# A transformer block on one core: ten units of QKV ahead and spilled, successive slots, turning by DMA, fp16 state

## The chip, the cores and the metric

The kernel runs on one core of a Trainium2 chip. Its time is the device time of one launch in microseconds, the median of several runs.

## What is computed

x has 4 sequences of 1024 tokens of 512 values. The reference, cut:

```python
x = x + layernorm(attn(layernorm(x)))
x = x + layernorm(ffn(layernorm(x)))

def attn(x):                       # 16 heads of 32, chunks of 128 tokens
    q, k, v = heads(x @ w_qkv.T + b_qkv)
    for each chunk:                # the state S is 32 x 32 a head
        inter  = (q * decay_q) @ S
        intra  = ((q @ k.T) * dmask) @ v
        S      = lam_c * S + (k * decay_k).T @ v
    return (inter + intra) @ w_out.T + b_out

def ffn(x):                        # weights rounded to fp8 e4m3
    return (silu(x @ gate * gate_s) * (x @ up * up_s)) @ down * down_s
```

## The kernel before

The tokens go in 16 units of 256 (two tiles of 128, `t`, or two chunks, `c`). Every wide product is made of fp16 halves: a number is a high half (written by ScalarE) and a low half (the number less the high half, written by GpSimd or VectorE), and three (two where the weights are rounded) fp16 matmuls are added in PSUM.

Each engine has its own program, written out by hand as a list of calls, and semaphores order them. `start` does unit 0's attention, unit 1's QKV and all the weights' preparation: VectorE rounds 12 pieces of 128x1536 to fp8 values (`magic`, L915 and L917; `rounded`, L922 and L924), and TensorE sums their squares (L496). Then `slot(s)` does three things at once: attention and out-projection of unit s, FFN of unit s-1, QKV of unit s+1. Slots 1 to 14 are of this kind; slot 15 has no QKV, slot 16 only the FFN of unit 15. A sequence is four units.

A slot on TensorE, in order (`slot`, L646): x1 of unit s-1 turned by 8 f32 transposes (L654); scores (L552), carry (query times state, f32, L565) and state (f32, L569) of chunk 0; gate and up (`gate_up`, L513) in six steps of 32 matmuls, with the other scores, `attend` (L583, L585), chunk 1's carry and state, and the turning of the next x (L441) between them; QKV's q and k (L621) with the turning of o (L595); out-projection (L603), down (L528) and V (L635); the turning of k (L644). PSUM banks, q and k (f32) and the state stay in place from one user to the next.

SyncE's list (`slot`, L274): load of the next x, stores, and `stack` (L253), which puts high and low halves of q and k on top of each other in `stacks` by 32 copies within SBUF (L261). GpSimd's list: low halves of the probabilities (L771), of h (L758), of q and k (L776) and of v (L784), the inverse standard deviations (L709, L712), the residuals (L793, L805), the decay of the f32 state of 128x512 (L765).

## Time and profile before

| | us |
|---|---|
| median of 3 runs (lowest, highest) | 1132.33 (1130.96, 1132.65) |
| the profiled execution | 1132.8 |
| its span | 1131.0 |
| TensorE busy | 1046.4 |
| VectorE, GpSimd, ScalarE busy | 733.5, 585.1, 391.6 |

The span runs from the first to the last profiled instruction. Busy times are of the span; matmuls overlap, so a block of them is best read as the distance from its start to the next block's start. A slot is the distance from one turning of x1 to the next.

### The profile page before, as it was taken

The numbers are of one execution on the slowest core, as the hardware profiler recorded it, in microseconds if no ns is written. First come the engines' busy times: TensorE is split into PE (matmuls) and PEld (weight loads), VectorE is DVE, ScalarE is ACT, GpSimd is POOL, SyncE is SP. The second block draws the span as 40 slices with busy tenths as digits, with TensorE's granted clock in tenths as the row PEclk, the third lists the DMA queues.
The fourth block names the chain that finished last, engine by engine and source line by source line (L and its number), as shares of the span: only waits on it lengthen the run. The fifth ranks groups of instructions, "written<-read, shape, count | busy, mean of one in ns | idle before, by whom it ended". The sixth has DMA issues, their size and how long they took to land.

```text
span 1131.0 us, 23001 instructions
## 1 busy us (share of the span) xinstructions
PE 1046.4 (93%) x8772; PEld 792.4 (70%) x8772; DVE 733.5 (65%) x1427; ACT 391.6 (35%) x752; POOL 585.1 (52%) x647
## 2 busy tenths in 40 slices
PE   1738689999999999999999999999999999999887
PEld 1537277786959687786959596786959596877654
DVE  7979984757657474756657474757667484746642
ACT  3324244251524233252424243342514243342211
POOL 0123454655656474655647474645556464656433
PEclk9867889999999999999999999999999999999989
DMA  9311501303040312213040312213040402112000
GB/s 364 105 65 57 122 1 36 77 16 89 11 103 12 69 45 50 66 22 82 11 103 11 74 39 55 61 27 77 13 101 11 86 28 59 55 38 58 1 19 19
DMA packets 83626, 66.09 MB, mean 58 GB/s; under 512 B 9280, under 2 KB 70848, under 8 KB 83392
## 3 DMA queue, kind: packets, MB, share of 16 engines
q1 hardware_dynamic: 82656, 64.00, 21.8%
q8 instruction: 75, 1.23, 0.5%
q10 hardware_dynamic: 864, 0.61, 0.2%
q14 instruction: 31, 0.25, 0.1%
HBM read 24.72 MB, written 8.39 MB: 29 GB/s over the span
## 4 chain that ended last, share of the span: by engine, by line
PE 84%; DVE 12%; issue 2%; POOL 1%; DMA 0%; POOLq 0%; ACT 0%; DVEq 0%; SPq 0%
PE bank L513 30%; PE bank L528 14%; PE bank L621 13%; PE bank L603 7%; PE bank L635 6%; PE bank L565 3%; PE bank L569 2%; PE bank L552 2%; PE bank L583 2%; DVE ffn_pool L922 2%; PE bank L654 1%; PE bank L441 1%; PE bank L644 1%; PE bank L595 1%; DVE ffn_pool L915 1%
## 5 line engine op out<-in xcount | busy, mean ns | idle before, releaser
L771 POOL TENSOR_TENSOR att_pool<-p,att_pool 128x512 f16<-128x512 f32 x128 | 148.1, 1178 | 80.8 <-ACT att_pool L371 80.8
L513 PE MATMUL bank<-ffn_pool,gate_q 128*128 128x256 f16 x1536 | 185.1, 274 | 3.8 <-DVE ffn_pool L1194 3.8
L513 PE MATMUL bank<-ffn_pool,up_q 128*128 128x256 f16 x1536 | 184.6, 274 | 0.0
L621 PE MATMUL bank<-x_hl,wqkv_hi 128*128 128x256 f16 x1024 | 171.3, 274 | 14.1 <-DVE wqkv_lo L906 14.1
L528 PE MATMUL bank<-down_q,ffn_pool 128*128 128x512 f16 x768 | 170.6, 379 | 1.0 <-DVE ffn_pool L1084 1.0
L513 PEld LDWEIGHTS bank<-ffn_pool,gate_q 128*128 128x128 f16 x1536 | 148.8, 98 | 21.5 <-DVE ffn_pool L1194 4.2
L513 PEld LDWEIGHTS bank<-ffn_pool,up_q 128*128 128x128 f16 x1536 | 151.0, 98 | 18.1
L758 POOL TENSOR_TENSOR ffn_pool<-ffn_pool 128x512 f16<-128x512 f32 x96 | 111.1, 1157 | 94.4 <-ACT ffn_pool L385 92.9
L371 ACT CAST att_pool<-p 128x512 f16<-128x512 f32 x128 | 77.9, 618 | 191.7 <-DVE p L1074 191.7
L1084 DVE SCALAR_TENSOR_TENSOR ffn_pool<-bank,us_t,ffn_pool 128x256 f32<-128x256 f32 x192 | 84.1, 480 | 89.4 <-PE bank L513 87.3
L621 PE MATMUL bank<-x_hl,wqkv_lo 128*128 128x256 f16 x512 | 140.5, 274 | 0.0
L528 PEld LDWEIGHTS bank<-down_q,ffn_pool 128*128 128x128 f16 x768 | 75.1, 98 | 91.6 <-DVE ffn_pool L1084 1.3
L776 POOL TENSOR_TENSOR att_pool<-qk,att_pool 128x512 f16<-128x512 f32 x60 | 71.1, 1186 | 116.0 <-ACT att_pool L351 116.0
L621 PEld LDWEIGHTS bank<-x_hl,wqkv_hi 128*128 128x128 f16 x1024 | 99.2, 98 | 27.5 <-issue 15.0
L357 ACT CAST v_hl<-v 128x512 f16<-128x512 f32 x32 | 19.8, 619 | 253.1 <-DVE v L1147 253.1
L1074 DVE TENSOR_TENSOR p<-bank,mask 128x512 f32<-128x512 f32 x128 | 83.5, 684 | 33.6 <-POOL att_pool L771 33.6
L379 ACT ACTIVATE ffn_pool<-bank,gs_t 128x256 f32<-128x256 f32 x192 | 80.3, 468 | 64.7 <-PE bank L513 64.7
L603 PE MATMUL bank<-wout_hl,o_t 128*128 128x512 f16 x384 | 91.6, 391 | 5.4 <-DVE o_t L1141 5.4
L709 POOL TENSOR_TENSOR rstd<-mv,eps_t 128x1 f32<-128x1 f32 (+1 forms) x112 | 23.3, 208 | 139.0 <-DVE mv L982 139.0
L346 ACT ACTIVATE qk<-bank,bqk 128x256 f32<-128x256 f32 x128 | 53.7, 470 | 89.9 <-PE bank L621 89.9
L635 PE MATMUL bank<-wqkv_hi,x_hl 128*128 128x512 f16 x256 | 76.1, 379 | 0.0
L1158 DVE SCALAR_TENSOR_TENSOR y<-bank,o_scale,bo 128x512 f32<-128x512 f32 x32 | 23.9, 748 | 80.5 <-PE bank L603 80.5
(123 smaller groups left out, 1658.9 us busy)
## 6 DMA issues: line engine op xcount, KB each, us to landing
att_pool<-att_pool SPq DMA_DIRECT2D x480, 64.0 KB, 2.1
x_t<-in_x SPq DMA_DIRECT2D x16, 512.0 KB, 3.5
out_x<-ffn_pool SPq DMA_DIRECT2D x32, 256.0 KB, 2.1
att_pool<-in_w_qkv_t SPq DMA_DIRECT2D x4, 768.0 KB, 8.1
ffn_pool<-in_gate_w SPq DMA_DIRECT2D x4, 768.0 KB, 12.9
ffn_pool<-in_up_w SPq DMA_DIRECT2D x4, 768.0 KB, 4.2
ffn_pool<-in_down_w SPq DMA_DIRECT2D x4, 768.0 KB, 4.6
mask<-in_mask_c SPq DMA_DIRECT2D x1, 1024.0 KB, 17.0
```

The lines of the kernel that those rows point to most:

```text
L371: nc.scalar.copy(pr_hl[:, 0, heads(s, g)], by_head(p32[:, g % 2])).then_inc(p_hi_d, 1)
L379: ins = nc.scalar.activation(sil[:, j], b_gate[:, j * TOK:(j + 1) * TOK], ACT.Silu, scale=gs_t[:, 2 * i + j:2 * i + j + 1])
L513: ins = nc.tensor.matmul(b[:, j * TOK:(j + 1) * TOK], w[:, k, o * P:(o + 1) * P], x1_hl[:, part, k], start=(k == 0 and part == 0), stop=(k ...
L528: ins = nc.tensor.matmul((b_gate, b_up)[t][:, :], h_hl[:, part, k, t * P:(t + 1) * P], down_q[:, k], start=(k == 0 and part == 0), stop=(k ...
L603: ins = nc.tensor.matmul((b_y, b_att)[c][:, :], o_t[:, c, a, k], wout_hl[:, b, k], start=(k == 0 and n == 0), stop=(k == KT - 1 and n == 2))
L621: ins = nc.tensor.matmul(b_t[i % 2][:, j * TOK:(j + 1) * TOK], (wqkv_hi, wqkv_lo)[a][:, k, o * P:(o + 1) * P], x_hl[:, b, k], start=(k == ...
L635: ins = nc.tensor.matmul(b_t[t][:, :], x_hl[:, b, k, t * P:(t + 1) * P], (wqkv_hi, wqkv_lo)[a][:, k, 2 * D:3 * D], start=(k == 0 and q == ...
L758: nc.gpsimd.tensor_tensor(h_hl[:, 1, 2 * i:2 * i + 2].rearrange("p k t -> p (k t)"), h32[:, i % 2], h_hl[:, 0, 2 * i:2 * i + 2].rearrange( ...
L771: nc.gpsimd.tensor_tensor(pr_hl[:, 1, heads(s, g)], by_head(p32[:, g % 2]), pr_hl[:, 0, heads(s, g)], ALU.subtract).then_inc(p_lo_d, 1)
L776: nc.gpsimd.tensor_tensor(qk_hl[:, 1, 2 * i:2 * i + 2].rearrange("p k t -> p (k t)"), qk[:, 2 * i:2 * i + 2].rearrange("p k t -> p (k t)") ...
L1074: nc.vector.tensor_tensor(by_head(p32[:, g % 2]), by_head(b_s[g % 2][:, :]), mask[:, heads(s, g)], ALU.mult).then_inc(p_d, 1)
L1084: ins = nc.vector.scalar_tensor_tensor(out=h32[:, i % 2, j * TOK:(j + 1) * TOK], in0=b_up[:, j * TOK:(j + 1) * TOK], scalar=us_t[:, 2 * i ...
```

## The change

- **QKV ahead.** `LEAD = 10`: the QKV products of units 0 to 9 are made first (`ahead(k)`), the other six in slots 0 to 5 (unit s+10 in slot s). Fp16 halves of q, k, v and of v times its decay go to DRAM (`spill_qk`, `spill_v`) and are loaded a slot before their use (`load_stacks`, `load_kt`, `load_v`). The rounding of the weights (`ROUNDED`) runs beside units 0 to 7.
- **Successive slots.** Slot s has the attention of unit s, the out-projection of unit s-1 (and its norms, residual, x1), the FFN of unit s-2. There are 18 slots. Slots 0 and 1 have no FFN (`early`), slots 6 to 15 no QKV, slots 16 and 17 no attention. The loop over sequences is written out.
- **Turning by DMA.** x, o, x1 and k are turned as fp16 halves by DMA transposes that SyncE issues: 128 rows of 1024 fp16 numbers (256 KB) each, two for x, o and x1, one of 512 KB for k. The f32 transposes on TensorE, and the PSUM copies behind them, go. Low halves of x and x1 are now made by GpSimd (two instructions of 128x512 each), also v times its decay and its low half (two each).
- **Fp16 state.** The state is 128x4x32, is scaled and split into halves (`state_scaled`, `state_hi`, `state_lo`), sent to DRAM and read back stacked in four pieces (`move_state`) before the next chunk's carry. Carry is 16 fp16 matmuls of 32 columns, state 12 of 128 columns.

```diff
...
+        dram_qk = nc.dram_tensor("dram_qk", [units, 2, 2, KT, P, TOK], F16, kind="Internal").ap()
+        dram_v = nc.dram_tensor("dram_v", [units, T, P, 4 * D], F16, kind="Internal").ap()
+        dram_s = nc.dram_tensor("dram_s", [2, P, 2 * P], F16, kind="Internal").ap()
...
+        ROUNDED = {0: (0,), 1: (1,), 2: (2, 3), 3: (4, 5), 4: (6,), 5: (7, 8), 6: (9,), 7: (10, 11)}
...
-                    for j in range(HG):
-                        for r in range(4):
-                            sp.dma_start(stacks[DH * r:DH * (r + 1), which, j::HG, :],
-                                         qk_hl[DH * j:DH * (j + 1), parts[r], KT * which:KT * (which + 1), :]
-                                         ).then_inc(done, 16)
...
+            def turn_o(s):
+                for t in range(T):
+                    sp.wait_ge(o_lo_d, 2 * s + t + 1)
+                    if t == 0:
+                        sp.wait_ge(*((out_mm, 2 * s) if s else (v_mm, 2 * LEAD)))
+                    sp.dma_start_transpose(turned(o_t[:, :, :, :].rearrange("p s k t -> p (s k) t"), t),
+                                           hl_1[:, t].rearrange("p s d -> p (s d)")).then_inc(o_turned, 16)
...
+            def spill_v(n, t):
+                sp.wait_ge(vd_lo_d, 2 * n + t + 1)
+                sp.dma_start(dram_v[n, t], vv[:, t]).then_inc(v_spilled[t], 16)
+
+            def load_stacks(s):
+                sp.wait_ge(q_spilled, 32 * (s + 1))
+                sp.wait_ge(k_spilled, 32 * (s + 1))
+                if s:
+                    sp.wait_ge(score_mm, 8 * s)
+                    sp.wait_ge(carry_mm, carries(s, 0))
...
+                for which, parts in ((1, (0, 0, 1, 1)), (0, (0, 1, 0, 1))):
+                    for r in range(4):
+                        sp.dma_start(stacks[DH * r:DH * (r + 1), which],
+                                     dram_qk[s, which, parts[r]].rearrange("g (j d) t -> d (g j) t", d=DH)
+                                     ).then_inc(stack_in, 16)
...
+            def load_v(s):
...
+                if s:
+                    sp.wait_ge(att_mm, 2 * s)
+                    sp.wait_ge(state_mm, states(s, 0))
...
+                sp.dma_start(vva, dram_v[s].rearrange("t p c -> p t c")).then_inc(v_in, 16)
+
+            def move_state(s, c):
+                if not has_state(s, c):
+                    return
+                n = states(s, c)
+                sp.wait_ge(state_lo_d, n + 1)
+                sp.dma_start(dram_s[n % 2], state_hl[:, :].rearrange("p s g e -> p (s g e)")).then_inc(state_out, 16)
+                sp.wait_ge(state_out, 16 * (n + 1))
+                at_least(sp, carry_mm, carries(s, c + 1) if has_carry(s, c) else carries(s, c))
+                for r in range(4):
...
+            for k in range(LEAD):
+                ahead(k)
+            load_stacks(0)
+            load_kt(0)
+            load_v(0)
...
+                if n < units:
+                    if s:
+                        turn_x(n)
+                    spill_v(n - 1, 0)
+                    spill_v(n - 1, 1)
+                    if n + 1 < units:
+                        load_x(n + 1)
...
+                if attends:
+                    move_state(s, 0)
+                if v >= 1:
+                    store(v - 1, 1)
+                if attends:
+                    load_xr(s)
+                if v < 0 and n < units:
+                    spill_qk(n, 0)
+                if s + 1 < units:
+                    load_stacks(s + 1)
+                    load_kt(s + 1)
+                if 0 <= u < units:
+                    turn_x1(u)
+                if attends:
+                    move_state(s, 1)
+                if s + 1 < units:
+                    load_v(s + 1)
...
+                if attends:
+                    turn_o(s)
...
+            def carry_and_state(s, c):
+                if c == 0:
+                    pe.wait_ge(v_d, 2 * min(units, LEAD + s))
+                    pe.wait_ge(kt_in, 16 * (s + 1))
+                    pe.wait_ge(v_in, 16 * (s + 1))
...
+                if has_carry(s, c):
+                    pe.wait_ge(state_in, 64 * states(s, c))
...
+            def slot(s):
+                n, u, v = s + LEAD, s - 1, s - 2
+                attends, projects = s < units, u < units
+                if attends:
+                    scores(s, 0, 0)
+                    carry_and_state(s, 0)
+                gate_up(v, 0)
+                if projects:
+                    project(u, 0)
+                    project(u, 1)
+                if attends:
+                    scores(s, 0, 1)
+                gate_up(v, 1)
+                gate_up(v, 2)
+                if attends:
+                    attend(s, 0)
+                    scores(s, 1, 0)
+                gate_up(v, 3)
+                if attends:
+                    scores(s, 1, 1)
+                    carry_and_state(s, 1)
+                gate_up(v, 4)
+                gate_up(v, 5)
+                if attends:
+                    attend(s, 1)
+                down(v, 0)
+                if n < units:
+                    for i in range(4):
+                        project_qk(n, i)
+                    project_v(n, 0)
+                    project_v(n, 1)
+                down(v, 1)
...
```

**Place 1: VectorE and GpSimd while QKV runs ahead.** VectorE before, in `start` (`v` is the sum of V and its bias, `gate_q` a rounded piece, `small` maxima):

```order
L922 TENSOR_TENSOR ffn_pool<-ffn_pool 128x1536
L924 TENSOR_TENSOR gate_q<-ffn_pool 128x1536
L915 TENSOR_SCALAR ffn_pool<-ffn_pool 128x1536
L917 TENSOR_SCALAR ffn_pool<-ffn_pool 128x1536
L1147 TENSOR_TENSOR v<-bank,bv 128x512 x2
L922 TENSOR_TENSOR ffn_pool<-ffn_pool 128x1536
L924 TENSOR_TENSOR gate_q<-ffn_pool 128x1536
L915 TENSOR_SCALAR ffn_pool<-ffn_pool 128x1536
L917 TENSOR_SCALAR ffn_pool<-ffn_pool 128x1536
```

VectorE now, in `ahead(2)`:

```order
L1154 TENSOR_SCALAR ffn_pool<-ffn_pool 128x1536
L1158 TENSOR_TENSOR ffn_pool<-ffn_pool 128x1536
L1160 TENSOR_TENSOR gate_q<-ffn_pool 128x1536
L1221 TENSOR_SCALAR xr<-xr,mv,rstd 128x512 x2
L1152 TENSOR_SCALAR ffn_pool<-ffn_pool 128x1536
L1154 TENSOR_SCALAR ffn_pool<-ffn_pool 128x1536
L1158 TENSOR_TENSOR ffn_pool<-ffn_pool 128x1536
L1160 TENSOR_TENSOR gate_q<-ffn_pool 128x1536
L1237 TENSOR_TENSOR v<-bank,bv 128x512 x2
```

GpSimd now, in `ahead(2)` (`qk_hl`, `vv`, `hl_x` are low halves, L897 multiplies v by its decay):

```order
L886 TENSOR_TENSOR qk_hl<-qk,qk_hl 128x512
L895 TENSOR_TENSOR vv<-v,vv 128x16x32
L897 TENSOR_TENSOR v<-v,decay_k 128x512
L886 TENSOR_TENSOR qk_hl<-qk,qk_hl 128x512
L895 TENSOR_TENSOR vv<-v,vv 128x16x32
L897 TENSOR_TENSOR v<-v,decay_k 128x512
L864 TENSOR_TENSOR rstd<-mv,eps_t 128x2
L867 TENSOR_TENSOR rstd<-rstd,eps_t 128x2
L886 TENSOR_TENSOR qk_hl<-qk,qk_hl 128x512
L901 TENSOR_TENSOR vv<-v,vv 128x512 x2
L886 TENSOR_TENSOR qk_hl<-qk,qk_hl 128x512
L881 TENSOR_TENSOR hl_x<-xr,hl_x 128x512 x2
```

The same rounding now stands between the norms of x, and 12 GpSimd instructions of 512 columns stand beside each unit of QKV.

**Place 2: SyncE in a slot.** Before, a slot of the loop (x of the next unit, the store, the stacking of q, then of k):

```order
L277 ISA [waits x1_d]
L277 DMA x_t<-in_x 128x2x512
L266 REGISTER_ALU
L267 ISA [waits fin_d]
L267 DMA out_x<-ffn_pool 128x512
L271 ISA
L256 ISA [waits stored]
L261 DMA att_pool<-att_pool 32x4x256 [waits qk_lo_d,qk_hi_d]
L261 DMA att_pool<-att_pool 32x4x256 x15
L261 DMA att_pool<-att_pool 32x4x256 [waits qk_lo_d,qk_hi_d]
L261 DMA att_pool<-att_pool 32x4x256 x15
```

Now, slot 4, its first part (turning of x, spill of v, load of x, `move_state(4, 0)` in L345 and L350, store, x for the residual):

```order
L278 DMA_TRANSPOSE x_hl<-hl_x 128x8x128 [waits v_mm,x_lo_d]
L278 DMA_TRANSPOSE x_hl<-hl_x 128x8x128 [waits x_lo_d]
L307 DMA dram_v<-vv 128x2048 [waits vd_lo_d] x2
L268 DMA x_q<-in_x 128x2x512 [waits x_lo_d]
L345 DMA dram_s<-state_hl 128x256 [waits state_lo_d]
L350 DMA state_st<-dram_s 32x4x128 [waits carry_mm,state_out]
L350 DMA state_st<-dram_s 32x4x128 x3
L362 DMA out_x<-ffn_pool 128x512 [waits fin_d]
L358 DMA xr<-in_x 128x2x512 [waits fin_d]
```

and its second part (stacks, k, x1, `move_state(4, 1)`, v, o):

```order
L319 DMA att_pool<-dram_qk 32x16x256 [waits score_mm,carry_mm,k_spilled,q_spilled]
L319 DMA att_pool<-dram_qk 32x16x256 x7
L327 DMA_TRANSPOSE kt<-dram_qk 128x2x1024 [waits state_mm]
L295 DMA_TRANSPOSE ffn_pool<-hl 128x8x128 [waits up_mm,x1_lo_d]
L295 DMA_TRANSPOSE ffn_pool<-hl 128x8x128 [waits x1_lo_d]
L345 DMA dram_s<-state_hl 128x256 [waits state_lo_d]
L350 DMA state_st<-dram_s 32x4x128 [waits carry_mm,state_out]
L350 DMA state_st<-dram_s 32x4x128 x3
L338 DMA vv_pool<-dram_v 128x2x2048 [waits att_mm,state_mm,v_spilled1,v_spilled0]
L287 DMA_TRANSPOSE o_t<-hl 128x8x128 [waits out_mm,o_lo_d]
L287 DMA_TRANSPOSE o_t<-hl 128x8x128 [waits o_lo_d]
```

The loads of the next unit and the turning stand in one list with the two trips of the state.

**Place 3: GpSimd ahead of the spill of v.** Before, the end of slot 1 (L784 are the low halves of v, in the slot that projects them):

```order
L793 TENSOR_TENSOR x<-x_t,y 128x512
L709 TENSOR_TENSOR rstd<-mv,eps_t 128x1
L712 TENSOR_TENSOR rstd<-rstd,eps_t 128x1
L709 TENSOR_TENSOR rstd<-mv,eps_t 128x1
L712 TENSOR_TENSOR rstd<-rstd,eps_t 128x1
L805 TENSOR_TENSOR ffn_pool<-x,ffn_pool 128x512
L709 TENSOR_TENSOR rstd<-mv,eps_t 128x1
L712 TENSOR_TENSOR rstd<-rstd,eps_t 128x1
L793 TENSOR_TENSOR x<-x_t,y 128x512
L709 TENSOR_TENSOR rstd<-mv,eps_t 128x1
L712 TENSOR_TENSOR rstd<-rstd,eps_t 128x1
L784 TENSOR_TENSOR v_hl<-v,v_hl 128x16x32 x2
```

Now, slot 3, up to the low halves of the decayed v of unit 12 (`vd_lo`, L901), which SyncE's L307 waits for (L953 and L939 residuals, L933 probabilities, L947 h):

```order
L953 TENSOR_TENSOR ffn_pool<-xr,ffn_pool 128x512
L864 TENSOR_TENSOR rstd<-mv,eps_t 128x1
L867 TENSOR_TENSOR rstd<-rstd,eps_t 128x1
L933 TENSOR_TENSOR att_pool<-p,att_pool 128x512 x2
L947 TENSOR_TENSOR ffn_pool<-ffn_pool 128x512
L939 TENSOR_TENSOR xr<-xr,y 128x512 x2
L864 TENSOR_TENSOR rstd<-mv,eps_t 128x1
L867 TENSOR_TENSOR rstd<-rstd,eps_t 128x1
L947 TENSOR_TENSOR ffn_pool<-ffn_pool 128x512
L864 TENSOR_TENSOR rstd<-mv,eps_t 128x1
L867 TENSOR_TENSOR rstd<-rstd,eps_t 128x1
L901 TENSOR_TENSOR vv<-v,vv 128x512 x2
```

V's low halves move from the end of their slot into the next slot, behind the third low half of h.

## Rows read from the trace of the kernel before

**Rows 1.** The page: busy time and share of the span; the main DMA queue.
```profile
PE 1046.4 (93%) x8772; PEld 792.4 (70%) x8772; DVE 733.5 (65%) x1427; ACT 391.6 (35%) x752; POOL 585.1 (52%) x647
q1 hardware_dynamic: 82656, 64.00, 21.8%
```

**Rows 2.** Windows: us, busy of PE, PEld, DVE, ACT, POOL (instructions), PEclk, DMA share, GB/s.
```profile
27.70:146.00 118.30, 75.85 (x483) 52.28 (x481) 108.50 (x129) 37.81 (x49) 40.68 (x33) 0.75 0.29 84
463.80:526.90 63.10, 63.07 (x545) 48.27 (x546) 38.65 (x83) 22.85 (x46) 34.47 (x40) 1.00 0.22 52
```

**Rows 3.** Windows, TensorE only (us, busy, PEclk, DMA share, GB/s), block by block.
```profile
463.83:464.75 0.92, 0.92 (x8) 1.00 0.10 29
464.75:465.20 0.45, 0.45 (x11) 1.00 0.00 0
465.20:466.14 0.94, 0.94 (x11) 1.00 0.00 0
466.14:467.18 1.04, 1.04 (x11) 1.00 0.03 8
467.18:470.68 3.50, 3.50 (x33) 1.00 0.02 5
478.11:478.99 0.88, 0.88 (x35) 1.00 0.73 272
500.06:505.30 5.24, 5.24 (x51) 1.00 0.20 41
505.30:507.88 2.58, 2.58 (x14) 1.00 0.50 102
507.88:513.07 5.19, 5.19 (x26) 1.00 0.50 101
```

**Rows 4.** Timeline, TensorE: the first QKV matmuls (start, length, idle before).
```profile
23.75 0.58 PE L621 MATMUL bank<-x_hl,wqkv_hi 128*128 128x256 f16 x2 [12.96 <-DVE wqkv_lo L906]
```

**Rows 5.** Single lines: duration min/median/max in ns.
```profile
L776 POOL TENSOR_TENSOR att_pool<-qk,att_pool x60: 1152/1156/2057, 105.2 to 1011.6; 128x512 f16<-128x512 f32 x60
L985 DVE TENSOR_SCALAR nrm<-x_t,mv,rstd x32: 537/540/1371, 7.7 to 986.8; 128x512 f32<-128x512 f32 x32
```

**Rows 6.** Timeline, GpSimd and VectorE in the same stretch.
```profile
111.09 2.05 POOL L776 TENSOR_TENSOR att_pool<-qk,att_pool 128x512 f16<-128x512 f32 x1 [2.11 <-ACT att_pool L351]
113.71 2.06 POOL L776 TENSOR_TENSOR att_pool<-qk,att_pool 128x512 f16<-128x512 f32 x1 [0.57 <-ACT att_pool L351]
110.37 1.75 DVE L922 TENSOR_TENSOR ffn_pool<-ffn_pool 128x1536 f32<-128x1536 f32 x1
112.15 2.60 DVE L924 TENSOR_TENSOR down_q<-ffn_pool 128x1536 f16<-128x1536 f32 x1
114.87 1.72 DVE L915 TENSOR_SCALAR ffn_pool<-ffn_pool 128x1536 uint32<-128x1536 uint32 x1
116.62 0.96 DVE L917 TENSOR_SCALAR ffn_pool<-ffn_pool 128x1536 f32<-128x1536 f32 x1
```

**Rows 7.** SyncE's issues L261 and landing of L261, then landing of L277.
```profile
L261 SPq DMA_DIRECT2D att_pool<-att_pool x480: 585/601/1908, 115.3 to 1027.2; - x160
DMA to landing us min/median/max: 2.0/2.1/5.0
DMA to landing us min/median/max: 3.4/3.5/4.4
```

**Rows 8.** Timeline, GpSimd in the steady slot: probabilities' low halves, an inverse deviation.
```profile
468.44 2.27 POOL L771 TENSOR_TENSOR att_pool<-p,att_pool 128x512 f16<-128x512 f32 x2 [4.47 <-ACT att_pool L371]
...
516.98 0.19 POOL L709 TENSOR_TENSOR rstd<-mv,eps_t 128x1 f32<-128x1 f32 x1 [2.33 <-DVE mv L982]
517.25 0.54 POOL L712 TENSOR_TENSOR rstd<-rstd,eps_t 128x1 f32<-128x1 f32 x1
```

**Rows 9.** The chain of waits at the end: start, length, what.
```profile
1088.51 24.01 PE bank L513 x192
1124.07 0.70 DVE ffn_pool L1179
```

1601 lines of the change are left out of this document (869 added, 732 removed).

## The prediction

> **What bounds the kernel now.** I read the page first, for the engine with the largest share: TensorE, 93% [rows 1]. Then the windows. From 27.7 to 146.0 us it is VectorE that is full (108.5 of 118.3 us) and TensorE works at a granted clock of 0.75; in a steady slot TensorE is busy 63.07 of 63.10 us at 1.00, with VectorE at 38.65 and GpSimd at 34.47 [rows 2]. So 14 slots are TensorE's own time, and the start is VectorE's rounding of weights. The chain of waits at the end has the FFN of unit 15 alone: 24.01 us for its gate and up (192 matmuls), and 6.9 us from the end of down (1124.07) to the span's 1131.0 [rows 9]. The change must be judged by what it takes from 63.1, and by the waits that its longer way through DRAM brings.
>
> **TensorE's work.** Per unit, four f32 turnings of about 0.9 us go: -3.6 (the stretch from 463.83 for one) [rows 3]. Carry and state, 0.94 and 1.04 in f32, twice a unit (3.8 with the second pair's shorter state, 0.9), become 16 matmuls of 32 columns (half of `attend`'s 32 in 0.88: 0.44) and 12 of 128 columns (8 take 0.45: 0.67), so 2.2: -1.6 [rows 3]. A slot with everything is then 63.1 - 3.6 - 1.6 = 57.9 us; of it QKV is 2 x 5.24 + 5.19 = 15.7, so a slot without QKV is 42.2. Sixteen units are 926 us; before they were 1010. This gain of 83 us and the start's idle time are what the waits below are set against.
>
> **Start.** The first QKV matmul stood at 23.75, behind the low half of the weights [rows 4]. Ahead of that VectorE loses two low halves of x and a first `magic` (some 3.1 us with L915 and L917 at 0.96 [rows 6]) and gains two moments of x (1 us beyond what a wait hid): 21.6.
>
> **Ten units ahead.** TensorE needs 15.7 us each. GpSimd has 12 instructions of 512 columns a unit at 1.16 [rows 5]: 13.9. VectorE rounds twelve pieces in units 0 to 7 (1, 1, 2, 2, 1, 2, 1, 2), each 0.96 + 0.96 + 1.75 + 1.76 = 5.4, and normalises twice a unit, 2 x 0.54 [rows 5, 6]. These do not run side by side. At 111.09 a GpSimd instruction of 1.16 takes 2.05 beside L922, L924 takes 2.60 in place of 1.76 beside it, and at 113.71 and 114.87 the same again (2.06, and L915 1.72 for 0.96): each waits for the other's end [rows 6]. So a unit takes 13.9 + 1.1 + 5.4 per piece: 20.4 with one, 25.8 with two, 22.7 in unit 4, where the split of W_out (2048 columns, 2.3 at L922's pace) is added. Unit 0 has no V work and waits for the weights: 18; units 8 and 9 are TensorE's 15.7. Sum: 18 + 20.4 + 25.8 + 25.8 + 22.7 + 25.8 + 20.4 + 25.8 + 15.7 + 15.7 = 216. The bounds are 159 (no mutual waiting) and 240 (GpSimd idle 2 to 3 us a unit besides). The Trainium skill (SBUF — State Buffer, Who interferes with whom) counts a VectorE instruction with two SBUF inputs, as L922, as shut out by a GpSimd read too; L922's row beside GpSimd shows no stretch of its own, since it had begun first. If L922 were free of it, the stage would be 12 x 1.75 = 21 us shorter.
>
> **SyncE's list is the new path.** A plain copy costs SyncE 0.60 and lands in 2.1; one of 512 KB lands in 3.5, so 1 MB in about 5.1 [rows 7]. A turning is not in the trace. Its nearest rows are L261's: 0.60 as median, 1.91 as the longest; below 0.60 nothing excludes a little. I take 1.25, the middle, for 256 KB and 2.5 for k's 512 KB. The Trainium skill (Advanced Engine Details and Errata, X-Bar Transpose (TRN2)) has such DMAs as fast as plain ones; with 0.60 the sum below is some 13 us less. Against it stands the table in DMA: Bandwidth & Descriptors (Why a DMA increments its semaphore by 16 and not by 1): before the newest generation the issuing sequencer pushed one command a tile, 32 cycles each; with 64 tiles in a turning (16 rows by 128 numbers, my count) and SyncE's 1.2 GHz from the same skill that is 1.7 us and the fixed part, about 2 us, an estimate, and the sum is 30 us higher. No row here shows either.
>
> **The loads of the next slot (slots 7 to 15).** `load_stacks` may go once carry of chunk 1 has read the stacks. From there: 8 x 0.60 = 4.8, k 2.5, x1's turnings 2.5, the state out 0.4 + 2.1 and back 4 x 0.60 (4.9), v 0.4 + 5.1: 20.2 us. TensorE has left: state 0.7, two steps of 3.5, `attend` 0.9, down 10.4, the next scores 0.45: 19.4 [rows 3]. So v comes 0.8 late where chunk 1 has a state (7 of 9 slots).
>
> **The state within a slot (slots 2 to 6).** There SyncE can send the state of chunk 0 only after `spill_v`, which waits for `vd_lo`, late in GpSimd's list. GpSimd is through with the first probabilities at about 4.4 (before, at 470.71, 5.5 after the scores' end at 465.20, less the 1.3 of x1's low halves on VectorE, more 0.2 since down's eviction now stands first [rows 3, 8]). Up to the end of `vd_lo` stand 14 instructions of 1.16 (16.2), five inverse deviations of 0.8 (4.0), the state's two small ones and hand-overs (1.0 by estimate) [rows 5, 8]: 21.2, so 25.6. Then SyncE: 0.5 + 0.4 + 0.4, landing 2.1, 4 x 0.60, landing 2.1: 33.5. TensorE is at carry of chunk 1 at 0.45 + 1.1 + 3.5 + 5.2 + 0.45 + 7.0 + 0.9 + 0.45 + 3.5 + 0.45 = 23.0 [rows 3]. It waits 10.5. Queued behind carry are the rest of the FFN and QKV; VectorE and GpSimd wait for these. Bounds: 0 (GpSimd early) and 14.
>
> **Slots 0 to 2.** Slot 0: its stacks, k and v are asked for behind q and k of unit 9: casts 1.5 + 1.2, spills 1.2, stacks 4.8, k 2.5, v 5.5 = 16.7, against V's 5.2 and the scores: a wait of 11; the state's trip, as above, 9; work 21: 41. Slot 1: x of unit 11 is turned at the end of SyncE's list (4.8 + 2.5 + 4.9 + 0.4 + 1.2 + 2.5 + 2.5 + 2.1 = 20.9 after carry, TensorE has 5.7): 15.2; state 2.5; work 26.6: 44.3. Slot 2: v is 20.2 after carry, TensorE has 4.7: 15.5; state 9; work 57.9: 82.4.
>
> **The sum.** 21.6 + 216 + 41 + 44.3 + 82.4, slots 3 to 5 3 x 68.4 = 205.2, slot 6 42.2 + 10.5 = 52.7, slots 7 to 15 9 x 42.2 + 7 x 0.8 = 385.4, slot 16 (FFN, out-projection) 36.6, slot 17 31.4, the end 6.9: 1123.5. After long waits TensorE comes back at the lower clock: the last unit's gate and up took 24.01 where six steps of 3.50 are 21.0 [rows 3, 9]. Nine waits of 8 us or more, 3 us each: 27. That is 1150.5 as a span; the median of before lies 1.3 over the span of its profiled execution: **1152**. So the 83 us of work and some 20 at the old start are given back as waits.
>
> **Rivals.** (1) *The run-ahead goes at TensorE's pace*, 18 + 9 x 15.7 = 159, because GpSimd's and VectorE's instructions mostly miss each other. For it: GpSimd has 13.9 of 15.7 to do, and L776's median over 60 is 1.156. Against: most of those stood beside instructions that read PSUM; the two beside the rounding took 2.05 and 2.06 [rows 5, 6]. Time 1152 - 57 = 1095, faster. The point: if the ten units take under 196 us, the kernel is faster than before. (2) *Nothing waits*: besides, states and loads are there in time: 21.6 + 159 + 21 + 26.6 + 4 x 57.9 + 10 x 42.2 + 36.6 + 31.4 + 6.9 = 957. Against: the trip of the state is two landings and six issues long whatever GpSimd does. (3) *Turnings are dear*: each further us on SyncE adds 4 us in seven slots and 12 in slots 0 to 2, 40 in all; at 1.91, 1178, and with the clock lost in those seven slots 1195; at 2.5, 1220. (4) *The change turns its DMA engines into the bound.* 64 MB took 21.8% of 16 engines, 247 us [rows 1]; now a unit moves 8 to 9 MB, 33 us of a 58 us slot, and 3 MB, 12 us, per unit ahead. It would need twice that price; I count it with (3).
>
> **How the numbers follow.** Forecast 0.42 (1125 to 1175), (1) 0.22, (2) 0.07, (3) with (4) 0.24, of that 0.06 above 1240; the rest, 0.05, is partial cover between (1) and (2). The range 1075 to 1240 leaves out (2), the dearest turnings, and a little between. A measurement here tells 0.2% (2.3 us) from no change. Faster: (1), (2) and the rest, 0.34; same 0.03, from the forecast's lower end; slower 0.63.
>
> **What the new profile would show.** The tenth unit's V ending near 238, with GpSimd instructions of 2 us beside the rounding and TensorE idle in each of units 1 to 7; if near 180, (1) holds. In slots 3 to 6, one gap of about 10 us on TensorE ahead of carry of chunk 1, ended by a DMA into `state_st`; if none, the order on GpSimd was mis-read. In slots 8 to 15 gaps under 2 us ahead of the state matmuls; if 5 or more, turnings cost over 2 us. SyncE's transposes give their price directly. A slot without QKV of 42 us of busy time confirms the ledger. The forecast is wrong as a whole if the gaps ahead of carry are absent and the run-ahead is at TensorE's pace.

## The result

The changed kernel is slower, and by much more than forecast.

| | before | after |
|---|---|---|
| median, us | 1131.67 (4 runs) | 1273.45 (4 runs, 1269.99 to 1277.33) |
| after / before, 95% interval | | 1.1253 (1.1219 to 1.1287) |
| span of the profiled execution | 1131.0 | 1268.2 |
| forecast (range) | | 1152 (1075 to 1240) |

The forecast had 20 us more, the chip shows 142. The time lies outside the range. The lines of the page of after that answer to [rows 1], with the issues of SyncE's loads and their landing (KB each, median us):

```profile
PE 1003.2 (79%) x8500; PEld 711.6 (56%) x8500; DVE 679.1 (54%) x1227; ACT 431.0 (34%) x816; POOL 746.0 (59%) x830
...
q1 hardware_dynamic: 283184, 163.12, 52.5%
...
PE 44%; POOL 18%; issue 10%; SPq 8%; DVE 7%; ACT 6%; DMA 6%; POOLq 0%; DVEq 0%; ACTq 0%
...
att_pool<-dram_qk SPq DMA_DIRECT2D x128, 256.0 KB, 5.7
...
vv_pool<-dram_v SPq DMA_DIRECT2D x16, 1024.0 KB, 5.7
```

TensorE's work did fall, by 43 us of busy time, but it is busy 79% of the span and no longer 93%. The chain of what ended last, which was TensorE for 84% before, passes through GpSimd, SyncE and the DMAs for 32%. The bytes rose from 64 MB to 163.

By stage, windows of after (us, busy of PE, PEld, DVE, ACT, POOL, granted clock, DMA share, GB/s): ten units ahead, slots 0 to 2, slots 3 to 6, slots 7 to 15, and slot 8 alone, to be held against [rows 2].

```profile
22.70:278.30 255.60, 191.61 (x1236) 125.97 (x1236) 150.68 (x154) 111.55 (x192) 171.44 (x136) 0.86 0.51 151
278.30:482.40 204.10, 124.53 (x1092) 89.61 (x1091) 77.82 (x158) 59.48 (x115) 102.70 (x119) 0.77 0.65 152
482.40:753.30 270.90, 225.88 (x2000) 163.97 (x1998) 138.07 (x267) 92.61 (x181) 163.69 (x189) 0.92 0.51 120
753.30:1189.60 436.30, 392.51 (x3678) 283.19 (x3676) 268.47 (x565) 143.75 (x285) 271.99 (x336) 0.98 0.56 122
804.10:849.20 45.10, 42.62 (x402) 30.90 (x401) 29.74 (x65) 15.93 (x32) 30.83 (x40) 1.00 0.56 118
```

What TensorE waited for, in sum, times, longest (view of waits, TensorE):

```profile
PE bank L714 <- DMA state_st<-dram_s: 45.0, 6, 10.0
PE bank L714 <- issue: 43.6, 9, 12.0
PE bank L688 <- ACT qk L470: 34.4, 6, 9.5
PE bank L699 <- DMA att_pool<-dram_qk: 30.3, 3, 13.3
PE att L688 <- ACT qk L470: 27.2, 6, 6.9
```

L714 is carry, L688 V's product, L699 the scores. The second row, "issue", stands ahead of carry at a slot's start. TensorE's list waits there for V, the keys and the state, and it is the load of V that comes last: SyncE issues it at the end of the slot before. In slot 8 it was issued at 846.63 us, V's loads land 5.7 us after their issue (median), and slot 9's carry begins at 852.25. Where there is no second state to move, the wait is absent.

| stage | forecast | measured | of it waits |
|---|---|---|---|
| first QKV matmul | 21.6 | 22.7 | |
| ten units ahead | 216 | 255.6 | 61.6 ahead of V |
| slot 0, 1, 2 | 41, 44.3, 82.4 | 60.0, 57.8, 86.2 | 79.5 |
| slots 3 to 5 | 205.2 | 216.9 | 26.9 for the state |
| slot 6 | 52.7 | 54.0 | 7.4 for the state |
| slots 7 to 15 | 385.4 | 436.4 | 22.5 at the starts, 20.2 within |
| slots 16, 17, end | 74.9 | 78.6 | |
| clock after waits, as a lump | 27 | in the stages | |
| span | 1150.5 | 1268.2 | |

### The profile page after: what moved, and what is told of

The parts are those of the page before. It is cut to its first block, busy times and chain, and to the rows that moved or that the text cites. A ratio compares the mean times of both kernels' runs of the same rounds, so it can differ in the third digit from the quotient of the medians.

```text
span 1268.2 us, 21610 instructions
## 1 busy us (share of the span) xinstructions
PE 1003.2 (79%) x8500; PEld 711.6 (56%) x8500; DVE 679.1 (54%) x1227; ACT 431.0 (34%) x816; POOL 746.0 (59%) x830
## 3 DMA queue, kind: packets, MB, share of 16 engines
q1 hardware_dynamic: 283184, 163.12, 52.5%
## 4 chain that ended last, share of the span: by engine, by line
PE 44%; POOL 18%; issue 10%; SPq 8%; DVE 7%; ACT 6%; DMA 6%; POOLq 0%; DVEq 0%; ACTq 0%
PE bank L771 13%; PE bank L785 12%; PE bank L675 5%; PE att L748 5%; POOL att_pool L933 4%; PE bank L688 4%; POOL vv L895 3%; POOL v L897 3%; DMA dram_s<-state_hl 2%; SPq L319 2%; SPq L327 2%; POOL qk_hl L886 2%; DVE p L1243 2%; POOL vv L901 2%; PE att L675 2%
## 5 line engine op out<-in xcount | busy, mean ns | idle before, releaser
L771 PE MATMUL bank<-ffn_pool,gate_q 128*128 128x256 f16 x1536 | 196.7, 285 | 13.3 <-ACT ffn_pool L523 13.3
L933 POOL TENSOR_TENSOR att_pool<-p,att_pool 128x512 f16<-128x512 f32 x128 | 150.8, 1198 | 67.9 <-ACT att_pool L496 67.9
L771 PEld LDWEIGHTS bank<-ffn_pool,gate_q 128*128 128x128 f16 x1536 | 152.7, 102 | 42.2 <-ACT ffn_pool L523 20.0
L947 POOL TENSOR_TENSOR ffn_pool<-ffn_pool 128x512 f16<-128x512 f32 x96 | 111.2, 1158 | 97.9 <-ACT ffn_pool L529 97.9
L771 PEld LDWEIGHTS bank<-ffn_pool,up_q 128*128 128x128 f16 x1536 | 150.5, 98 | 22.5 <-DVE ffn_pool L1330 4.5
L675 PE MATMUL bank<-x_hl,wqkv_hi 128*128 128x256 f16 x704 | 124.6, 284 | 31.1 <-DVE wqkv_lo L1145 23.5
L496 ACT CAST att_pool<-p 128x512 f16<-128x512 f32 x128 | 76.9, 618 | 191.6 <-DVE p L1243 191.4
L785 PEld LDWEIGHTS bank<-down_q,ffn_pool 128*128 128x128 f16 x768 | 73.9, 98 | 99.2 <-DVE ffn_pool L1330 12.4
L886 POOL TENSOR_TENSOR qk_hl<-qk,qk_hl 128x512 f16<-128x512 f32 x64 | 80.2, 1256 | 83.1 <-ACT qk_hl L476 65.4
L864 POOL TENSOR_TENSOR rstd<-mv,eps_t 128x1 f32<-128x1 f32 (+1 forms) x112 | 27.9, 249 | 147.0 <-DVE mv L1218 136.6
L1243 DVE TENSOR_TENSOR p<-bank,mask 128x512 f32<-128x512 f32 x128 | 83.1, 681 | 50.1 <-PE bank L699 35.0
L529 ACT CAST ffn_pool<-ffn_pool 128x512 f16<-128x512 f32 x96 | 59.3, 617 | 128.9 <-DVE ffn_pool L1330 127.3
L675 PE MATMUL bank<-x_hl,wqkv_lo 128*128 128x256 f16 x352 | 99.8, 284 | 0.0
L675 PEld LDWEIGHTS bank<-x_hl,wqkv_hi 128*128 128x128 f16 x704 | 70.8, 102 | 46.8 <-issue 23.4
L688 PE MATMUL bank<-wqkv_hi,x_hl 128*128 128x512 f16 x176 | 64.6, 456 | 34.4 <-ACT qk L470 34.4
L714 PE MATMUL bank<-state_st,att_pool 128*128 128x32 f16 x448 | 15.8, 180 | 88.7 <-DMA state_st<-dram_s 45.0
L748 PE MATMUL att<-wout_hl,o_t 128*128 128x512 f16 x384 | 85.5, 379 | 0.0
L699 PE MATMUL bank<-att_pool 128*128 128x128 f16 x512 | 43.8, 226 | 40.6 <-DMA att_pool<-dram_qk 30.3
```

The costliest lines, as they stand in the source:

```text
L496: nc.scalar.copy(pr_hl[:, 0, heads(g)], by_head(p32[:, g % 2])).then_inc(p_hi_d, 1)
L675: ins = nc.tensor.matmul(qk_banks(n)[i % 2][:, j * TOK:(j + 1) * TOK], (wqkv_hi, wqkv_lo)[a][:, k, o * P:(o + 1) * P], x_mov(n)[:, b, k], ...
L688: ins = nc.tensor.matmul(qk_banks(n)[t], x_mov(n)[:, b, k, t * P:(t + 1) * P], (wqkv_hi, wqkv_lo)[a][:, k, 2 * D:3 * D], start=(k == 0 and ...
L748: ins = nc.tensor.matmul(b_y[t], o_t[:, a, k, t * P:(t + 1) * P], wout_hl[:, b, k], start=(k == 0 and n == 0), stop=(k == KT - 1 and n == 2))
L771: ins = nc.tensor.matmul(b[:, j * TOK:(j + 1) * TOK], w[:, k, o * P:(o + 1) * P], x1_hl[:, v % 2, part, k], start=(k == 0 and part == 0), ...
L785: ins = nc.tensor.matmul((b_gate, b_up)[t][:, :], h_hl[:, part, k, t * P:(t + 1) * P], down_q[:, k], start=(k == 0 and part == 0), stop=(k ...
```

## Experiments

All are the changed kernel with one or a few edits. Each row has two runs (four for `e30all` and `e96all`); the two of a kernel lie up to 7.9 us apart, so 4 us or less between kernels says nothing. The kernel before stood at 1131.3 to 1133.2 beside them. "Ahead" is the stage of the ten units, from the first QKV matmul to the last V.

| run | edit | us | against 1273.5 | ahead |
|---|---|---|---|---|
| e1 | ScalarE: fourth Q/K part first | 1250.7 | -22.8 | 228.9 |
| e2 | rounding left out | 1257.0 | -16.5 | 233.7 |
| e12 | both | 1220.4 | -53.1 | 195.7 |
| e18 | e1, and V's sum first on VectorE | 1246.3 | -27.1 | 227.2 |
| e20 | e18, and ScalarE's parts in a row | 1248.4 | -25.1 | 229.0 |
| e3 | state moved ahead of V's spill | 1264.9 | -8.6 | |
| e39 | e3, and half of the stacks from ScalarE | 1240.4 | -33.1 | |
| e37 | e3, and the FFN's input turned first | 1235.7 | -37.8 | |
| e4 | second key buffer from slot 6 on | 1255.3 | -18.1 | |
| e5 | unit 0's loads earlier | 1259.8 | -13.6 | |
| ekp | keys copied, not turned | 1263.8 | -9.6 | |
| epl | all turnings copies | 1256.2 | -17.3 | |
| e10 | half of the stacks' loads left out | 1227.7 | -45.8 | |
| e30 | stacks in 2 KB packets | 1271.6 | -1.9 | |
| eall | e1, e3, e4, e5, e37 | 1175.4 | -98.0 | 229.6 |
| eall2 | eall, e20's lists, earlier keys in slots 0, 1 | 1178.1 | -95.3 | 227.8 |
| e30all | eall and e30 | 1183.4 | -90.1 | 230.3 |
| e96all | eall, a quarter of the stacks' bytes less | 1159.9 | -113.6 | 230.3 |

### The ten units ahead

In after, TensorE stands ahead of the second half of V in units 0 to 8, for 4.2 to 9.5 us, and twice ahead of the first. Unit 4, timelines of ScalarE, VectorE, GpSimd and TensorE (start, length, idle before and what ended it):

```profile
149.67 0.62 ACT L486 CAST vv<-v 128x512 f16<-128x512 f32 x1 [5.56 <-POOL v L897]
153.56 0.62 ACT L463 CAST hl_x<-xr 128x512 f16<-128x512 f32 x1 [3.27 <-DVE xr L1221]
...
155.32 0.83 ACT L470 ACTIVATE qk<-bank,bqk 128x256 f32<-128x256 f32 x2
```

```profile
146.15 2.59 DVE L1158 TENSOR_TENSOR ffn_pool<-ffn_pool 128x1536 f32<-128x1536 f32 x1
148.77 2.48 DVE L1160 TENSOR_TENSOR up_q<-ffn_pool 128x1536 f16<-128x1536 f32 x1
152.11 2.65 DVE L1221 TENSOR_SCALAR xr<-xr,mv,rstd 128x512 f32<-128x512 f32 x2 [0.86 <-POOL rstd L867]
```

```profile
147.20 2.44 POOL L897 TENSOR_TENSOR v<-v,decay_k 128x512 f32<-128x512 f32 x1
149.60 1.70 POOL L864 TENSOR_TENSOR rstd<-mv,eps_t 128x2 f32<-128x2 f32 x1
151.39 0.69 POOL L867 TENSOR_TENSOR rstd<-rstd,eps_t 128x2 f32<-128x2 f32 x1
```

```profile
156.21 1.03 PE L688 MATMUL bank<-wqkv_hi,x_hl 128*128 128x512 f16 x2 [9.54 <-ACT qk L470]
```

ScalarE's list has the high half of a later input (L463) ahead of the fourth Q/K part (L470) that TensorE needs for the second half of V. L463 waits for VectorE's normalisation (L1221), which waits for GpSimd's deviation (L864, L867), which stands behind the low halves of V of the unit before and its product with the decay (L897, 2.44 us beside the rounding, L1160). The row ahead of L463 has a second wait of the same list: 5.56 us for that product. V's product, when it comes, starts the next turn of the same ring.

e1:

```diff
-                if k + 2 <= LEAD:
-                    x_hi(k + 2)
                 front(k, 3)
+                if k + 2 <= LEAD:
+                    x_hi(k + 2)
```

> Only ScalarE's list of the ten units ahead changes: the fourth part of the Q/K stage (front(k, 3)) comes ahead of the rounding of the second next unit's input (x_hi(k + 2)), not behind it. Theory, a ring of hand-overs: in the changed kernel TensorE waits 4 to 9.5 us in every unit ahead of the second half of V, and ends that wait with ScalarE's qk; ScalarE stands at x_hi, which waits for VectorE's normalised input, which stands behind a piece of rounding and GpSimd's 1/sigma. With the part put first, those waits go; ten units fall from 255.6 us to 215 to 230, and the time from 1273 to 1233 to 1248. Rival, the sum of VectorE's and GpSimd's work sets the pace (the basis of the forecast of 216 us for the stage, which the trace then missed by 40): the waits only move to another place of the unit, and the time stays within 5 us of 1273.

1250.65 us, just above what the ring's theory gave; the stage, 228.9, is within it. The rival's 1273 is excluded. The waits ahead of V did not all go: they fell from 61.6 to 41.5 us, and ScalarE's fourth part still ends them.

e2 replaces `magic` and `rounded` by one pass:

```diff
             def quant(n):
-                magic(n)
-                rounded(n)
+                dve.wait_ge(f_in[n % 3], 16 * (n // 3 + 1))
+                nc.vector.tensor_scalar(piece_out(n), f_stage[n % 3], 1.0, None, ALU.mult).then_inc(f_q_d, 1)
```

> The rounding of the twelve FFN weight pieces to 8-bit values is left out: each piece is only copied (one pass of VectorE in place of four), so the FFN is computed with unrounded weights. Some 6 to 8 us of VectorE work in each of twelve pieces go, all of them in the ten units ahead, and with them what the two-input passes hold up on GpSimd. Ring of hand-overs: unit 8, which has no piece, took 23.3 us in the changed kernel; the ten units fall from 255.6 to about 10 x 23 = 230 us, the time to about 1248. Rival, the sum of VectorE's and GpSimd's work: 12 x 7 = 84 us of the two engines' work gone, the stage falls to what TensorE itself needs there, 18 us a unit at the full clock, so to 180 to 195 us, and the time to 1200 to 1215.

1256.95, stage 233.7. VectorE's busy time in the stage fell from 150.7 to 83.1 us, and the stage by only 22. So the sum of the two engines' work, on which the forecast stood, did not set the pace of this kernel.

> Both edits of the first two runs together: ScalarE's fourth Q/K part ahead of the next input's rounding, and the rounding of the FFN weight pieces left out (the FFN runs on unrounded weights). Alone the first took 23 us off the time and the second 16.5, where 10 units still took 23.4 us each. If the ring of hand-overs is one ring with two sources of length (the place of x_hi and the pieces), both together take off more than their sum of 40 us: V's waits go wholly, the ten units fall to 185 to 200 us and the time to 1195 to 1215. If other hand-overs are just behind (low halves of V and K on GpSimd), the units stay at 21 to 22 us and the time at 1230 to 1240.

1220.4, stage 195.7: the two together take 53 us off and not 39. With the part in its new place, the rounding is worth 33 us of stage (228.9 to 195.7), in the old place 22. The time is 5 us above what the first theory gave (1195 to 1215), the stage within what it gave (185 to 200), and its claim of more than the sum holds.

e18 moves `v_sum` ahead of the second `quant`; e20 also orders ScalarE's list anew (put in short here):

```diff
+                for t in range(T):          # VectorE, e18 and e20
+                    v_sum(k, t)
                 for n in pieces[1:]:
                     quant(n)
...
+                v_hi(k - 1, 0); v_hi(k - 1, 1)      # ScalarE, e20: the whole list
+                front(k, 0); front(k, 1); front(k, 2); front(k, 3)
+                vd_hi(k - 1, 0); vd_hi(k - 1, 1)
+                x_hi(k + 2)
```

> The edit of e1, and VectorE's list of the ten units: the sum of V out of the PSUM (v_sum) comes ahead of the second piece of rounding, not behind it. In e1, unit 6, V's sum was made at 178.4 us although its product had ended at 169.4, because a piece stood in between; GpSimd's work on V then fell beside the next piece (1.87 and 2.44 us in place of 1.16 and 1.05) and ScalarE waited for it until 188.3. Theory, hand-overs in the wrong order: in the four units with two pieces 3 to 6 us of the waits go, the ten units fall from 229 to 210 to 217 us and the time from 1250 to 1233 to 1240. Rival, VectorE's and GpSimd's shared work: the piece is only put off and the time stays within 4 us of 1250.

> The ten units ahead with all four hand-overs in another order, nothing left out: on ScalarE V's high halves of the unit before first, then the four Q/K parts in a row, then the high halves of decayed V and of the next input; on VectorE V's sum ahead of the second piece of rounding. In the run with V's sum first and x_hi last (227 us for the ten units) ScalarE still stood 5.4 us a unit ahead of the fourth part, at the high half of decayed V, which waits for GpSimd. Theory, a ring of hand-overs in the lists' order: with the part ahead of it 3 to 5 us go in 8 units, 227 to 190 to 205 us, and the time to 1210 to 1225. Rival, the two engines' sum with its mutual waiting, which the forecast had at 216: the stage stays at 220 or above and the time above 1238.

1246.3 and 1248.4, stages 227.2 and 229.0: both theories of a ring that goes on in other places fall. The waits only moved, as the rivals said. The windows of e1 and e12 over this stage, then e1 and e20 over its middle:

```profile
22.90:251.80 228.90, 184.91 (x1236) 124.29 (x1236) 161.10 (x155) 111.52 (x192) 178.78 (x136) 0.91 0.56 168
```

```profile
23.00:218.90 195.90, 173.41 (x1236) 121.42 (x1236) 83.74 (x119) 110.81 (x192) 143.82 (x136) 0.97 0.67 198
```

```profile
95.00:232.00 137.00, 109.63 (x739) 74.27 (x738) 108.31 (x90) 68.73 (x117) 120.28 (x83) 0.90 0.61 181
```

```profile
95.00:232.00 137.00, 109.46 (x742) 73.86 (x741) 107.18 (x91) 68.94 (x117) 122.37 (x82) 0.90 0.63 180
```

The same GpSimd instructions take 143.8 us without rounding and 179 beside it. In the middle of the stage GpSimd is busy for 88 and 89% in e1 and e20; in after it was 75% (114.2 of 153.0 us from 96 to 249). Three orders end within 2 us of each other, with GpSimd nearly full; that its work, stretched by the rounding, sets the pace there fits this and e12, but no run shows it alone. Open are the last 11% of GpSimd's time, and what holds ScalarE's fourth part back in e12, where TensorE is busy 173.4 of 195.7 us and still waits 20.2 for that part.

### The state within a slot

e3:

```diff
+                if n < units and s:
+                    turn_x(n)
+                if attends:
+                    move_state(s, 0)
                 if n < units:
-                    if s:
-                        turn_x(n)
                     spill_v(n - 1, 0)
                     spill_v(n - 1, 1)
...
-                if attends:
-                    move_state(s, 0)
```

> Only SyncE's list in the slots changes: the first move of the state out to DRAM and back comes ahead of the spill of V, not behind it. Theory, the queue: in slots 3 to 5 of the changed kernel the state's two halves were ready at 493.0 us, but SyncE stood at the spill of V until 509.4, moved the state out at 510.3 and back at 514.1, and TensorE waited 9.4, 10.0 and 7.5 us for it, 7.4 in slot 6 and 9.5 in slot 2. With the move put first the state is back before TensorE asks: slots 2 to 6 lose 7 to 10 us each, the time falls by 35 to 45 us to 1228 to 1238, and the slots 3 to 5 take 61 to 64 us in place of 71 to 73. Rival, another wait is right behind (GpSimd ends the low halves of the probabilities at 511.8 to 516.2, beside the state): only 1 to 4 us a slot go, and the time stays above 1255.

1264.9, in the rival's range, but not by the rival's mechanism. The waits for the state are gone from slots 3 to 6. Slots 3 to 5 took 72.7, 73.9 and 68.6 us, 1.7 less in sum than in after; only slot 6, which has no QKV, fell by 5. In the others the gain was given back some 30 us further on. The next slots gave back some too: slot 7 took 54.2 us for 50.9. e3, slot 3, timelines of SyncE's queue, ScalarE and TensorE:

```profile
504.31 10.30 SPq L319 DMA_DIRECT2D att_pool<-dram_qk  x8
514.65 5.04 SPq L327 DMA_TRANSPOSE kt<-dram_qk  x1
519.78 3.81 SPq L295 DMA_TRANSPOSE ffn_pool<-hl  x2
```

```profile
525.60 1.33 ACT L510 ACTIVATE hl<-o,o_scale 128x512 f16<-128x512 f32 x2 [13.29 <-DMA ffn_pool<-hl]
```

```profile
530.25 0.61 PE L675 MATMUL bank<-x_hl,wqkv_hi 128*128 128x256 f16 x2 [7.93 <-ACT qk L470]
```

ScalarE may write attention's output only when the FFN's input, in the same buffer `hl_1`, has been turned, and SyncE turns that behind stacks and keys. ScalarE's Q/K parts stand behind it in its list.

> The edit of e3 (state moved ahead of V's spill), and from slot 2 on the four loads of the next unit's Q stacks are issued by ScalarE, which waits 13 us there, and not by SyncE. e3 took the waits of 7 to 10 us for the state away, but slots 3 to 5 stayed at 72 us: TensorE then waited 7.9, 5.9 and 2.3 us for the Q/K stage, because ScalarE could not write attention's output until SyncE had turned the FFN's input, issued at 519.8 us, 10 us after it was ready, behind 10.3 us of stack loads and a 5.0 us key turning. Theory, SyncE's issue time bounds the slots: with 4 to 5 us fewer on it the turning comes 4 to 5 us earlier, slots 3 to 5 fall to 67 to 69 us, and in slots 7 to 15 the load of V comes earlier and the waits of 2.4 to 4.4 us at the slot's start go; the time falls from 1265 to 1230 to 1240. Rival, the DMA engines and not the issuing engine set how long those loads take (52% of the DMA time is in use): the issue only moves and the time stays within 6 us of 1265.

```diff
+                    for r in range(4):      # ScalarE, behind h_hi(v, 5)
+                        nc.scalar.dma_start(stacks[DH * r:DH * (r + 1), 0], ...
```

1240.4, and two answers. The waits at the starts of slots 7 to 15 fell from 27.1 us in e3 to 9.5, of which 7.4 are slot 7's (slots 9 to 14 took 45.1 to 47.0 us). Slots 3 to 5 hardly moved (72.6, 70.9, 69.3), because the issues behind the stacks became longer (by 5.9 us) as the stacks' became shorter (by 7.4):

```profile
504.62 2.94 SPq L321 DMA_DIRECT2D att_pool<-dram_qk  x4
507.61 8.23 SPq L329 DMA_TRANSPOSE kt<-dram_qk  x1
515.93 6.49 SPq L295 DMA_TRANSPOSE ffn_pool<-hl  x2
```

The rival's reason holds there: it is not who issues. The Trainium skill (DMA: Bandwidth & Descriptors, Issuing engines are not separate DMA queues) has both issuing engines' copies go through the same sixteen DMA engines; this row agrees. Letting ScalarE issue the turning was not tried, since by the Trainium skill (DMA: Bandwidth & Descriptors, Silent corruption: two transposing streams in flight at once) two engines' turnings under way together can spoil each other's data; no run here shows it.

e37 only changes the place:

```diff
+                if 2 <= s < 6:
+                    turn_x1(u)
                 if s + 1 < units:
                     load_stacks(s + 1)
                     load_kt(s + 1)
-                if 0 <= u < units:
+                if 0 <= u < units and not 2 <= s < 6:
                     turn_x1(u)
```

> The edit of e3 (state moved ahead of V's spill), and in slots 2 to 5 SyncE turns the FFN's input before it loads the next unit's stacks and keys, not behind them. With ScalarE issuing half of the stacks' loads (e39) slot 3 stayed at 72.6 us: the stacks' issues fell to 2.9 us but the key turning rose from 5.0 to 8.2 us and that of the FFN's input from 3.8 to 6.5, and the input was turned at 522.4 us as before. Theory, the turning stands behind data that the DMA engines still move, so its place in the order counts and not who issues: put first it is done at about 515, ScalarE writes attention's output at 516 and not at 526, the wait of 4 to 8 us for the Q/K stage goes, slots 3 to 5 fall from 73, 74 and 69 us (e3) to 66 to 68, and the time from 1265 to 1245 to 1252; the stacks then come 5 to 8 us later, which the 28 us from there to the slot's end hide. Rival, the end of attention itself or the store of the FFN bounds those slots: they stay at 71 to 73 us.

1235.7, more than expected; slots 3 to 5 took 64.6, 64.9 and 65.0 us. What TensorE waited for in them, e37:

```profile
PE bank L773 <- ACT ffn_pool L525: 8.7, 6, 2.6
PE bank L701 <- DVE p L1245: 3.0, 6, 0.8
```

So the state's trip and the turning's place were the whole of the DMA waits there. e3 alone had removed the first and run into the second.

### Keys, loads, turnings, bytes

> From slot 6 on, the key table has a second buffer (in the space of the input tile that is free by then), and SyncE turns the next unit's keys early in the slot, while it is idle, not behind the stacks in the slot's second half. Theory, the issue time of the 512 KB turning (4.4 to 6.8 us on SyncE) delays the load of V: the load of V is issued 5 to 6 us earlier, the waits of 2.4 to 4.4 us at the start of slots 7 to 15 (seven of them, 22.5 us in sum) go, and the time falls by 15 to 23 us to 1250 to 1258. Rival, the load of V waits for the second half of attention anyway (TensorE ends it some 4 us before the slot's end) and its landing takes 5.7 us: the waits shrink by under 1 us each, and the time stays above 1266.

```diff
+        def kt_of(s):
+            if s > 6 and s % 2:
+                return x_q ...          # as fp16; free from slot 6 on
+            return kt[:, :]
...
+                if 6 <= s < units - 1:
+                    load_kt(s + 1)      # early in the slot, behind load_xr(s)
...
```

1255.3, in the theory's range. The waits at the starts of slots 7 to 15 fell from 22.5 us to 10.2 and did not go.

> SyncE's list: the loads of unit 0's stacks, keys and values come ahead of the last ahead-unit's spills, not behind all of them. In the changed kernel TensorE waited 13.3 us for the stacks and 4.1 us for V at the start of slot 0, since the loads were issued at 279.7 us, behind the last spill, and take 6.1, 5.4 and 0.5 us to issue. Theory, SyncE's order: both waits go, 15 to 18 us off the time of 1273 (to 1255 to 1258). Rival, the 12 us of issues now stand ahead of the last spills and stop ScalarE and TensorE in the last ahead-unit instead: under 5 us off.

```diff
             for k in range(LEAD):
                 ahead(k)
+                if k == LEAD - 2:
+                    load_stacks(0)
+                    load_kt(0)
+                    load_v(0)
```

1259.8. The wait for the stacks (13.3) went, that for V (4.1) fell to 3.1, and a later one (for the probabilities' low halves) rose from 5.2 to 7.3: 13.6 in all, a little under what was expected.

Then the price of a turning. `ekp` loads the keys by a plain copy of the same bytes, `epl` makes all turnings such copies:

```diff
-                sp.dma_start_transpose(kt[:, :].rearrange("p t s d -> p t (s d)"),
-                                       dram_qk[s, 1].rearrange("s g p t -> (s g p) t")).then_inc(kt_in, 16)
+                sp.dma_start(kt...rearrange("p (a b) -> p a b", b=TOK),
+                             dram_qk[s, 1].rearrange("s g p t -> p (s g) t")).then_inc(kt_in, 16)
```

> Only the keys' load changes: 512 KB a unit come by a plain copy and not turned, so attention's state is made with keys that are not turned. Theory, the turning's price on SyncE: 16 issues of 4.4 to 6.8 us become 16 of about 0.4; the load of V, behind it, is issued 5 us earlier; the waits of 2.4 to 4.4 us at the start of slots 7 to 15 go (22 us) and 4 to 6 us each in slots 0 to 2, so 32 to 40 us off 1273 (1233 to 1241). Rival, the volume bounds: the same bytes still move and the time falls by under 12 us.

> Every turning by DMA (x, attention's output, the FFN's input, the keys) becomes a plain copy of the same bytes; all products behind them are then of data that is not turned. It is the price of turning by DMA as a whole, beside copies of the same size. In the changed kernel SyncE spends 2.6 us on each pair of 256 KB turnings and 4.4 to 6.8 us on each of 512 KB: 16 x 5.5 + 48 x 2.6 = 213 us of its list, against 16 x 0.4 + 96 x 0.45 = 50. Theory, that list is on the path in all slots: beyond the keys alone (expected 1233 to 1241) another 15 to 30 us go, to 1205 to 1225, since x1's turning bounds slots 3 to 5 and x's that of slot 1. Rival, only the keys' turning is on the path: within 5 us of the run with the keys alone.

1263.8 and 1256.2: the rival is right for the keys (under 12 us), and everything else that is turned costs 8 us more. Another place for the keys' turning (e4) had brought 18 us, more than doing without it. SyncE's queue in slot 8, in after, in ekp and in epl:

```profile
828.45 5.24 SPq L319 DMA_DIRECT2D att_pool<-dram_qk  x8
833.74 6.24 SPq L327 DMA_TRANSPOSE kt<-dram_qk  x1
840.08 2.61 SPq L295 DMA_TRANSPOSE ffn_pool<-hl  x2
```

```profile
825.06 5.45 SPq L319 DMA_DIRECT2D att_pool<-dram_qk  x8
830.55 1.07 SPq L327 DMA_DIRECT2D kt<-dram_qk  x1
831.73 6.68 SPq L295 DMA_TRANSPOSE ffn_pool<-hl  x2
```

```profile
819.10 5.29 SPq L319 DMA_DIRECT2D att_pool<-dram_qk  x8
824.44 1.02 SPq L327 DMA_DIRECT2D kt<-dram_qk  x1
825.56 5.87 SPq L295 DMA_DIRECT2D ffn_pool<-hl  x2
```

The keys' issue falls by 5.2 us, and the pair behind it rises by 4.1. Even two plain copies of 256 KB take 5.87 us to issue there, where such a copy of x takes 0.60 as median in the same run. The three groups of issues together take 14.1, 13.2 and 12.2 us. So most of the 4.4 to 6.8 us of the key turning were not its own. By these rows they were the time until what stood ahead in the queue had drained.

> Only the loads of the Q stacks are left out after unit 0's (the scores and the carry of the later units use unit 0's Q): four of eight loads of 256 KB a unit go, 1 of some 4.5 MB that a slot moves; no turning changes. Theory, the volume behind the stacks: in the run with the keys copied plainly the turning of the FFN's input rose from 2.6 to 5.8 to 6.7 us as that of the keys fell from 5.5 to 1.1, so what SyncE's issues take there is the time in which its queue drains 2 MB of stacks, and the next issue waits for it. With half of the stacks the issues of stacks and keys together fall from 11.5 to about 6 us, the waits for stacks in slots 0 to 2 (13.3, 9.3, 7.7) and for V at the starts of slots 7 to 15 fall by 4 to 5 us or go: 1230 to 1240. Rival, the price is that of each turning by itself: the stacks' issues fall by 2.5 us, the key turning keeps its 5.2 to 6 us, and the time stays above 1255.

```diff
-                for which, parts in ((1, (0, 0, 1, 1)), (0, (0, 1, 0, 1))):
+                for which, parts in ((1, (0, 0, 1, 1)), (0, (0, 1, 0, 1)))[:1 if s else 2]:
...
```

1227.7, 45.8 us off, slightly more than the theory of the volume gave. The same three groups in slot 8 took 9.7 us for 14.1. With all turnings kept, the waits for stacks in slots 1 and 2 fell from 9.3 and 7.7 to 4.3 and 3.2, those for V in slots 7 to 15 went (a slot took 44.4 to 45.9). The two long waits for V at the starts of slots 1 and 2 (9.2 and 12.0 in after, 9.5 and 12.0 here) stayed, but behind a shorter wait for the stacks: V came 4.6 and 4.5 us sooner after the carry that opens the burst.

e30 asks whether it is packets or bytes:

```diff
-                    sp.dma_start(dram_qk[n, which, part].rearrange("k p t -> p k t"), qk_hl...)
+                    sp.dma_start(dram_h[n, which, part], qk_hl...)      # [P, KT, TOK]
...
-                                     dram_qk[s, which, parts[r]].rearrange("g (j d) t -> d (g j) t", d=DH)
+                                     dram_h[s, which, parts[r]].rearrange("(j d) g t -> d j (g t)", d=DH)
```

> Only the layout in DRAM changes: Q's and K's halves are spilled with 2 KB of a partition side by side (K also once more in the old layout, for its turning: 0.5 MB a unit more written), so that the eight loads of stacks move the same 2 MB a unit in 4096 packets' worth of 512 bytes before, now in a quarter as many packets of 2 KB. Halving the stacks' loads took 46 us off (1227.7) and the keys' plain copy only 10. Theory, the packets: the stacks' loads drain in half of the time or less, the issue of keys and input behind them shrinks, and most of the 46 us come: 1225 to 1245. Rival, the bytes: 2 MB take the same time in any packet size (and 0.5 MB more are written), the time stays within 8 us of 1273 or rises.

> The same layout together with the orders of the 1175 us run. There TensorE still waited 60.9 us in slots 0 to 2 (13.5 for stacks, 21.3 and 5.9 for V, 3.8 for the turned input), 13.1 for V in slots 7 to 15, and the ten units took 229.6. If the packets are what takes the time, the waits in slots 0 to 2 fall by 12 to 20 us and those of slots 7 to 15 by 8 to 12: 1145 to 1158, still above the 1131.7 of the kernel before. If the bytes are, it stays at 1170 to 1182.

1271.6, and 1183.4 (4 runs, 1181.2 to 1186.2) for eall with the same edit, which alone has 1175.4. The packets fell, the pages of after and of e30 say, and the time did not:

```profile
DMA packets 284005, 165.04 MB, mean 130 GB/s; under 512 B 157440, under 2 KB 259328, under 8 KB 283776
```

```profile
DMA packets 227175, 173.43 MB, mean 137 GB/s; under 512 B 157953, under 2 KB 177921, under 8 KB 226945
```

It is the bytes. What e30 writes more can't hide a gain in slots 7 to 15, where no unit is spilled: there the three groups take 15.0 us for 14.1 in slot 8, and the waits at the starts 22.0 for 22.5. Both runs write half a megabyte a unit more in the stages before, which may be why e30all is 8 us slower than eall; that was not taken apart.

### All orders together

> All orders of list together, nothing left out: ScalarE's fourth Q/K part first (e1, -23 us alone), state moved ahead of V's spill (e3, -9), second key buffer from slot 6 on (e4, -18), unit 0's loads ahead of the last spills (e5, -14), the FFN's input turned first in slots 2 to 5 (-15 to -20 by expectation). If the waits are independent the sum gives 1273 - 79 to 84 = 1190 to 1195, which is still 5% over the kernel before; if they share causes, 1205 to 1225. Nothing in the traces gives under 1180, so the kernel before stays the faster one.

1175.4 (1175.3 and 1175.5), 15 us better than the sum expected. That sum had 15 to 20 us for the turning's place; with the 29 that it brought in e37, the parts add up to 92 of the 98 us. Slots 3 to 5 take 63 to 65 us, slots 8 to 14 45.1 to 47.5, slot 7 53.2, and with fewer waits TensorE's granted clock is 0.95 over the span where after has 0.91. Stages of eall (ten units, slots 0 to 2, slots 3 to 6), against 255.6, 204.1 and 270.9 of after:

```profile
23.10:252.70 229.60, 183.20 (x1239) 123.95 (x1240) 160.94 (x154) 111.95 (x192) 178.97 (x136) 0.92 0.62 174
252.70:431.50 178.80, 117.42 (x1091) 85.90 (x1089) 77.28 (x158) 59.54 (x115) 102.67 (x119) 0.84 0.67 165
431.50:673.70 242.20, 223.75 (x2000) 161.74 (x1998) 135.41 (x264) 91.97 (x181) 163.92 (x189) 0.98 0.58 133
```

eall2 has e20's lists in place of e1's, and on SyncE:

```diff
+            if s == 1:                  # kt_of
+                return ffn_pool[:, 0:1024]...       # free until slot 2
...
-                if 6 <= s < units - 1:
+                if 6 <= s < units - 1 or s < 2:
                     load_kt(s + 1)
...
+                if s == 0:
+                    turn_x(n + 1)
                 if attends:
                     turn_o(s)
```

> All orders together (1175 us with ScalarE's and SyncE's simple ones), with the ahead lists of e20, and in slots 0 and 1 the next keys turned early into free buffers and unit 11's input turned ahead of attention's output. In the 1175 us run TensorE waited 8.0 us for stacks, 9.0 for V and 3.8 for the turned input in slot 1, and 5.6 and 12.3 in slot 2. Expected: 5.5 us off V's wait in each of the two, 3 to 4 off the input's, and 25 to 35 from the ahead stage if e20's theory holds: 1130 to 1145, level with the kernel before. If the sum of the two engines' work holds the stage at 220: 1155 to 1165.

1178.1: neither half of it did anything. Slots 0 to 2 took 178.8 us in both. V's waits in slots 1 and 2 fell by 1.5 and 2.9 us and others rose.

> The orders of the 1175 us run, and fewer bytes: scores and carry are made of three stacked parts (96 partitions: high x high, high x low, low x high) and not four, the low x low term is left out; six loads of 256 KB for the stacks in place of eight, three of 32 KB for the state in place of four. A layout with a quarter of the packets and the same bytes left the time as it was (1271.6 against 1273.5), so if bytes are what the queue drains, half a megabyte less a unit gives a quarter to half of what halving the stacks gave (46 us, where no wait was hidden yet): 8 to 20 us, so 1155 to 1167, most of it in slots 0 to 2. If not even bytes count any more behind the other orders, within 4 us of 1175. The kernel before, at 1131.6, stays faster by either.

```diff
-                for which, parts in ((1, (0, 0, 1, 1)), (0, (0, 1, 0, 1))):
-                    for r in range(4):
+                for which, parts in ((1, (0, 0, 1)), (0, (0, 1, 0))):
+                    for r in range(3):
...
```

1159.9 (4 runs, 1157.4 to 1165.4), 15.5 us under eall: bytes again, in the range given. The place was not: slots 0 to 2 gave 6 us, slots 7 to 15 about 10 (45.3 us a slot on average from slot 8 to 14, and 3.0 us at the starts for 13.1). Its ratio to the kernel before is 1.026 (1.0222 to 1.0298), so no version of this design that was run reaches the kernel before. It still has 230 us for ten units' QKV, which are 157 of TensorE's time at its pace, and 55 us of waits in slots 0 to 2.

## Why the prediction was wrong

**Right.** The direction. The ledger of TensorE: a slot without QKV was to be 42.2 us of work, and slot 8 is busy 42.62. The wait of 10 us for the state in slots 2 to 6, with its cause: measured 9.5, 9.4, 10.0, 7.5 and 7.4, and in slot 3 `vd_lo` ended 27.1 us after the slot's start for a forecast of 25.6. e3 shows that `spill_v` was the reason. A turning of 256 KB that has nothing ahead of it costs SyncE 1.24 to 1.3 us as median; 1.25 was taken. Source lines of after:

```profile
L278 SPq DMA_TRANSPOSE x_hl<-hl_x x22: 1235/1301/4083, 9.7 to 624.5; - x22
...
DMA to landing us min/median/max: 2.7/2.9/6.9
```

Of the signs, the gap ahead of carry of chunk 1 came as named; the waits at the starts of slots 7 to 15, 2.4 to 4.4 us each, lay between its two signs (under 2, and 5 or more).

The Trainium skill (Advanced Engine Details and Errata, X-Bar Transpose (TRN2)) calls such DMAs as fast as plain ones. Nearly so here: making all of them plain brought 17 us of 1273. The Trainium skill's other page weighed then (DMA: Bandwidth & Descriptors, Why a DMA increments its semaphore by 16 and not by 1), with a command a tile, is not borne out: the estimate from it was 1.7 us and a fixed part, about 2 us.

**Wrong (1): ten units ahead, 216 for 255.6.** The step that failed is the unit's cost as a sum of GpSimd's and VectorE's work. e2 shows it was not the pace: three quarters of the rounding's passes went and the stage fell by 22 us. A ring of hand-overs through ScalarE's list set it, for 27 us of the stage (e1). No row of that list was placed in time. With the part moved, the stage lies 13 us above the sum (three orders: 227 to 229), and there the sum's mechanism fits but is not shown by itself. Terms that were too small: `normalise_x` was counted at 2 x 0.54 and takes 2.65 in unit 4; L864 takes 1.70 in two of the ten units and 0.19 in the others; L1152 and L1154 take up to 1.9 and 1.8 for 0.96. Rival (1), the run-ahead at TensorE's pace (159), is excluded: even without rounding the stage is 196. A part of the miss may be the clock's: TensorE is busy 191.6 us in the stage for 157 by the ledger, at a granted clock of 0.86, and 173.4 at 0.97 in e12; no run separates it.

**Wrong (2): SyncE's list by prices of lone issues.** Stacks were 8 x 0.60 and a landing of 2.1, from copies of 64 KB [rows 7], where these have 256; they issue in 5.2 to 8.6 and land in 5.7 as median and 8.4 at most. Keys were 2.5 and take 4.4 to 6.8, with a landing of 8.2:

```profile
L327 SPq DMA_TRANSPOSE kt<-dram_qk x16: 4433/5472/6776, 285.9 to 1124.8; - x16
...
DMA to landing us min/median/max: 7.3/8.2/9.5
```

The step that failed is that each price was added to the next as if the queue were empty, while some 3.5 MB (stacks, keys, V) follow one another. That is rival (4), the DMA engines, which was judged by the mean over a slot (33 of 58 us) and folded into (3), dear turnings. The mean was near enough (52.5% of the span). The burst behind carry of chunk 1 is what counts, and it is the bytes: e10 took 46 us off with half of the stacks left out, e30 nothing with their packets cut to a quarter. In slot 8 the way from the first issue (828.45) to slot 9's carry takes 23.8 us for 20.2, and the keys' issue alone 3.7 more than its term. The waits of slots 7 to 15 at the starts are 22.5 for 5.6, which is 17 of the 51 missed there. In slots 0 to 2 the waits are 79.5 us for 62.2, and the forecast had named some wrongly: none for the stacks of slots 1 and 2 (9.3 and 7.7), 15.2 for x's turning in slot 1 (3.8, and 9.2 for V), 9 for the state in slot 0 (1.3, and 5.2 for the probabilities' low halves).

**Wrong (3): waits within a slot and the clock.** The sum for a slot had TensorE's work and the one great wait. 20.2 us of small hand-overs in slots 7 to 15 (up to 1.3 each, ahead of gate, up, down and the scores; ScalarE and VectorE end them) were not in it. The clock was a lump of 27. TensorE's busy time over the ledger's work is 19 us in slots 0 to 2 (124.5 for 105.5, granted clock 0.77), 10 in slots 3 to 6, 13 in slots 7 to 15, 42 without the stage ahead; in slot 8, at 1.00, it is 0.4. The stages' misses add up to 144.7, and less the lump of 27 they are the 117.7 between forecast and span.

**Slots 3 to 5** were missed by 11.7 only. That the wait was right there is partly luck: e3 shows a second wait, for the turning of the FFN's input, just behind the first, and the forecast named none. TensorE's own work was 10 us over the ledger there.

**The chances.** The range's upper end, 1240, rested on the turnings' price, 88 us above the forecast. The stage ahead (40 us), the queue's waits (17 and 17), the small hand-overs (20) and TensorE's longer work (42 for 27) were separate misses, and the range had room for one or two of them, not for all.

**Open.** The waits for V of 9 and 12 us at the starts of slots 1 and 2 stayed in every run: 9.2 and 12.0 in after, 8.9 and 11.3 in e96all. An earlier load of the keys did little for them (eall2); half of the stacks brought V sooner, but slot and wait then began sooner too (e10). Behind stacks and keys, V's load also stands behind the state's second trip (338.17 to 342.13 us in SyncE's list of slot 0). No run put it ahead of that trip. Why slot 7 begins with a wait of 7 us once the slots before it are shorter (e3, e37, e39, eall) is open too.

## What to carry to other kernels

When work is moved ahead, write down for every engine what stands in its list in front of the instruction that TensorE waits for, and follow it round: a copy for two units later, one line too early, cost 23 us here, and no sum of busy times showed it. Cost a queue of loads by the bytes that stand ahead of each one in its burst, not by the issue and landing of a lone copy nor by the mean DMA share. Where a wait is removed and the time stays, look further down the same slot for who took its place, and try both edits together: e3 alone gave 9 us, with its second half 38.

## What the runs showed of the hardware that was not expected

- **SyncE's issue time is elastic.** A load of 512 KB took 1.07 us to issue in place of 6.24 when not turned, and the next pair then took 6.68 in place of 2.61. The issue times behind the burst followed the bytes ahead (14.1 us for the three groups, 9.7 with half of the stacks), not the instruction.
- **512-byte packets cost no more than those of 2 KB** for the same 2 MB of stacks: 57,000 fewer packets, 1271.6 against 1273.5 us. In DMA: Bandwidth & Descriptors (Specifications) the Trainium skill has 512 bytes as the least transfer for the full rate; the run agrees.
- **Turning by DMA beside copying the same bytes**: 17 us for 96 turnings of 256 KB and 16 of 512 KB in 1273.
- **A GpSimd instruction of two columns took 1.70 us in place of 0.19** beside a VectorE instruction with two inputs in SBUF (149.60 beside L1160, above; 0.19 in eight of the ten units). The Trainium skill (SBUF — State Buffer, Who interferes with whom) says that such an instruction contends with a GpSimd one that reads SBUF; in e1, L1158 averages 2.38 us over its twelve, for 1.75 in the kernel before [rows 6], so it is stretched itself too. In the prediction this was left open.
